# Order of three VectorE instructions and of filler matmuls in the first sample of a 16-sample attention and graph kernel

## The reference

```python
x = x + attention(_gn(x), w_qkv, w_out, b_out, gn_weight, gn_bias)
x = x + graph(_gn(x), w1, b1, gamma1, beta1, w2, b2, gamma2, beta2)

# attention, 4 heads of 32 dimensions, N = 1024 tokens
q, k, v = split(einsum('oc,bcn->bon', w_qkv, x))
q = softmax(q, axis=-2) * scale        # over the 32 dimensions of a head
k = softmax(k, axis=-1)                # over the tokens
context = einsum('bhdn,bhen->bhde', k, v)
out = einsum('bhde,bhdn->bhen', context, q)
out = normalize(einsum('oc,bcn->bon', w_out, out) + b_out) * gn_weight + gn_bias

# graph: unit vectors per token, similarity of all tokens, top 9 neighbours,
# two rounds of (feat @ w, weighted sum over neighbours, group norm, silu)
```

## Time and profile before

| what | value |
|---|---|
| median of 3 runs | 694.48 us (687.77, 694.48, 695.98) |
| profiled execution | 693.69 us, its span 691.9 us |
| mean granted TensorE clock | 0.978 of full |
| TensorE busy | 623.0 us (90%) |
| VectorE busy | 536.2 us (77%) |
| GpSimd busy | 499.6 us (72%) |
| ScalarE busy | 449.3 us (65%) |

### The profile page before, as it was taken

How to read it: one execution, slowest core, us unless ns; L and a number is a source line. 1 busy time by engine, 2 the same in 40 slices (tenths; PEclk the granted TensorE clock), 3 DMA queues, 4 the chain that set the end, 5 groups by cost and what they waited for, 6 DMA issues and landing times.

```text
span 691.9 us, 12330 instructions
## 1 busy us (share of the span) xinstructions
PE 623.0 (90%) x3821; PEld 312.0 (45%) x3821; DVE 536.2 (77%) x1008; ACT 449.3 (65%) x942; POOL 499.6 (72%) x534
## 2 busy tenths in 40 slices
PE   7787979898999999998999999998989999889984
PEld 5563635344353535353444535353534444333441
DVE  2238788888898989888898889898888988857821
ACT  2236658586786878585867768786858687643321
POOL 0122787868787888888797978888887979786810
PEclk9999999999999999999999999999999999979997
DMA  3002343434354444435353535435343634454311
GB/s 93 0 17 46 71 83 78 91 71 107 83 102 84 100 85 93 92 83 102 76 110 77 108 76 107 85 86 103 83 96 71 108 63 101 82 96 88 62 32 31
DMA packets 148722, 55.76 MB, mean 81 GB/s; under 512 B 138008, under 2 KB 138512, under 8 KB 148656
## 3 DMA queue, kind: packets, MB, share of 16 engines
q1 hardware_dynamic: 148656, 54.97, 38.8%
HBM read 12.87 MB, written 4.32 MB: 25 GB/s over the span
## 4 chain that ended last, share of the span: by engine, by line
PE 31%; POOL 25%; issue 16%; DVE 10%; DMA 9%; ACT 7%; SPq 1%; POOLq 0%; ACTq 0%; DVEq 0%
PE pC L967 17%; POOL adj L389 10%; POOL adj L384 5%; PE pS L923 4%; DMA rbc<-rn_row 4%; DMA rn_row<-rnT 4%; POOL qn L348 3%; ACT adj L527 2%; PE pB L768 2%; POOL res L407 2%; DVE kstat L607 2%; ACT ek L458 2%; PE pA L807 2%; POOL xn L372 2%; DVE top L676 2%
## 5 line engine op out<-in xcount | busy, mean ns | idle before, releaser
L967 PE MATMUL pC<-adj,xt 128*64 128x512 f32 x992 | 233.2, 603 | 3.1 <-POOL adj L395 1.8
L389 POOL TENSOR_TENSOR adj<-maskT,adj 128x128 f32<-128x128 f16 (+3 forms) x127 | 163.6, 1288 | 28.2 <-DMA maskT<-mask 25.3
L676 DVE MAX8 top<-pS 128x8 f32<-128x1024 f32 x128 | 155.6, 1224 | 30.7 <-ACT adj L527 30.5
L694 DVE MATCH_REPLACE8 mask<-top,pS 128x1024 uint16<-128x1024 f32 x128 | 155.3, 1213 | 0.0
L923 PE MATMUL pS<-xn 64*128 64x512 f32 x256 | 145.3, 655 | 6.2 <-issue 5.6
L923 PE MATMUL pS<-xn,xsw 64*128 64x512 f32 x256 | 144.7, 656 | 2.9 <-DVE mask L694 2.9
L527 ACT COPY adj<-pS 128x1024 f32<-128x1024 f32 x128 | 128.3, 1004 | 27.3 <-PE pS L925 27.1
L384 POOL TENSOR_TENSOR adj<-maskT,adj 128x128 f32<-128x128 f16 (+6 forms) x111 | 128.5, 1158 | 0.0
L967 PEld LDWEIGHTS pC<-adj,xt 128*64 128x64 f32 x992 | 63.9, 137 | 103.6 <-issue 96.0
L395 POOL TENSOR_TENSOR adj<-adj,selves 128x128 f32<-128x128 f32 x127 | 58.7, 462 | 8.7
L925 PEld LDWEIGHTS pS<-mark,place 64*128 64x128 f16 x256 | 24.5, 96 | 76.1 <-issue 76.1
(11 more groups left out here) (153 smaller groups left out, 1101.7 us busy)
## 6 DMA issues: line engine op xcount, KB each, us to landing
xs<-x SPq DMA_DIRECT2D x32, 128.0 KB, 2.8
vbc<-v_row SPq DMA_DIRECT2D x32, 128.0 KB, 2.9
rbc<-rn_row SPq DMA_DIRECT2D x30, 128.0 KB, 2.8
xsw<-xn SPq DMA_DIRECT2D x30, 128.0 KB, 2.4
out<-res SPq DMA_DIRECT2D x30, 128.0 KB, 2.4
maskT<-mask SPq DMA_TRANSPOSE x128, 3.1
cst<-packed SPq DMA_DIRECT2D x1, 471.5 KB, 3.9
y1sw<-y SPq DMA_DIRECT2D x2, 128.0 KB, 2.3
```

What stands on the lines that cost most here:

```text
L389: pool.tensor_tensor(above, m[:, r, 0:r + 1, :].bitcast(F16), above, ALU.mult).then_inc(done["upper"], 1)
L676: dve.max(top[b % 2][:, r, 0:TOP], pS[r % 2][:, :]).then_inc(done["tile_top"], 1)
L694: dve.match_replace(out=mask[n % MASKS][:, :], in_to_replace=top[b % 2][:, r, 0:TOP], in_values=pS[r % 2][:, :], imm_value=ONE_BITS).then_ ...
L967: mm = pe.matmul(ps[h * C:(h + 1) * C, 0:H], xt[:, t % NJ, t // NJ, :], adj[b % 2][:, t, h * H:(h + 1) * H], start=(t == 0), stop=(t == NT ...
```

## The change

In sample 0 VectorE's mT (scaling of the keys' product) goes behind qsum and qrec of the queries; in all other samples the order stays. Fillers: 9 in place of 8 in front of the transposes of qn of sample 0 (qT), 18 in place of 20 in front of the product with yT (ky), 8 in place of 4 in front of the sums of squares (ss).

```diff
-("ekT", 0): 9, ("qT", 0): 8, ("att", 0): 7, ("at_mean", 0): 16
+("ekT", 0): 9, ("qT", 0): 9, ("att", 0): 7, ("at_mean", 0): 16
-("k", 1): 9, ("ss", 0): 4, ("att", 1): 6
+("k", 1): 9, ("ss", 0): 8, ("att", 1): 6
-("ky", 0): 20,
+("ky", 0): 18,
...
-                yield
-                dve.wait_ge(*of("m_ps", b))
-                dve.wait_ge(*of("k_rec", b))
-                dve.wait_ge(*of("att_ps", b - 1))
-                dve.tensor_scalar(mT[:, :], pB[:, 256:256 + C], kstat[:, 2:3], SCALE, ALU.mult, ALU.mult).then_inc(done["m_copied"], 1)
+                if b >= 1:
+                    yield
+                    dve.wait_ge(*of("m_ps", b))
+                    dve.wait_ge(*of("k_rec", b))
+                    dve.wait_ge(*of("att_ps", b - 1))
+                    dve.tensor_scalar(mT[:, :], pB[:, 256:256 + C], kstat[:, 2:3], SCALE, ALU.mult, ALU.mult).then_inc(done["m_copied"], 1)
                 yield
                 dve.wait_ge(*of("q_exp", b))
                 dve.tensor_reduce(qsum[:, :], qe[:, :, :], AX.X, ALU.add).then_inc(done["q_sum"], 1)
                 dve.wait_ge(*of("q_sum", b))
                 dve.wait_ge(*of("q_norm", b - 1))
                 dve.reciprocal(qrec[:, :], qsum[:, :]).then_inc(done["q_rec"], 1)
+                if b < 1:
+                    yield
+                    dve.wait_ge(*of("m_ps", b))
+                    dve.wait_ge(*of("k_rec", b))
+                    dve.wait_ge(*of("att_ps", b - 1))
+                    dve.tensor_scalar(mT[:, :], pB[:, 256:256 + C], kstat[:, 2:3], SCALE, ALU.mult, ALU.mult).then_inc(done["m_copied"], 1)
```

More of the change, by code:

```diff
@@ L74 @@
 WARM = {
-    ("start", 0): 36, ("k", 0): 20, ("ekT", 0): 9, ("qT", 0): 8, ("att", 0): 7, ("at_mean", 0): 16, ("in_mean", 1): 6,
-    ("mi_mean", 0): 32, ("k", 1): 9, ("ss", 0): 4, ("att", 1): 6, ("sim1", 0): 2, ("mi_mean", 1): 24, ("k", 2): 9,
+    ("start", 0): 36, ("k", 0): 20, ("ekT", 0): 9, ("qT", 0): 9, ("att", 0): 7, ("at_mean", 0): 16, ("in_mean", 1): 6,
+    ("mi_mean", 0): 32, ("k", 1): 9, ("ss", 0): 8, ("att", 1): 6, ("sim1", 0): 2, ("mi_mean", 1): 24, ("k", 2): 9,
     ("xt1", 1): 24, ("g1_mean", 14): 18, ("sim7", 15): 12, ("g2_mean", 14): 18, ("g1_mean", 15): 12, ("xt2", 15): 21,
-    ("a2_0", 15): 5, ("ky", 0): 20,
+    ("a2_0", 15): 5, ("ky", 0): 18,
 }
```

## The result

The changed kernel has a median of 687.32 us over 20 runs (683.81 to 691.00), the kernel before 692.97 us over 20 runs (687.77 to 696.16). The ratio is 0.9916 with a 95% interval of 0.9894 to 0.9937: a gain of 5.8 us on 693, between 4.4 and 7.3 (the two medians themselves differ by 5.65). The time lies in the predicted range and is within 2%. The forecast of the gain was 4.0, a little under that interval.

What follows compares the result with a forecast made beforehand. The start was taken as one chain in sample 0, its queries' side held behind mT. Terms of 2.95 and 1.07 us, filler edits taken as nothing, gave 4.02 us off 693.69: 689.7 us, range 685.0 to 694.5.

Steps and rivals of the forecast that it cites:

- The chain and the free engines: Start of sample 0: one chain, queries' side late behind mT, engines idle; attention matmul expected near 25.6 in place of 29.61.
- First term: Sample 0, transposes of qn: with qsum and qrec ahead of mT they start at 23.40, not 26.35, 2.95 us earlier.
- Second term: Sample 0, transposes to attention matmul: without TensorE's idle time, sample 1's 2.19 us in place of 3.26, 1.07 us gained.
- The rival built on it: Clock at sample 0's transposes: typical executions lack the second term, only 2.95 gained, 690.7 us (691.5 from the median); chance 0.15.
- Fillers ky: Sample 0, 20 to 18 fillers before a wait that is late anyway: nothing; a clock fall would bound the loss.
- Fillers ss and the broadcasts: Sample 0, 4 to 8 fillers before the sums of squares: between -0.1 and +1.5 us at the row broadcasts, taken as 0.
- the rival that had 0.12: Sample 0's row broadcasts: the clock holds there too, 1.5 us more gained, 688.2 us; chance 0.12.
- The sum: Attention matmul of sample 0: 2.95 + 1.07 = 4.02 us earlier, all reaching the end, 689.7 us.
- the main forecast: Whole kernel: 689.7 us with its own spread of 688.5 to 691; chance 0.45.
- The shift reaches the end whole: All later samples: the last sample should still be 4.0 us ahead, since later work hangs on sample 0's attention matmul.
- The slower rival: Aggregation and similarity of a late sample, and one more place: new clock falls cost 4.4 us, 694.1 us; chance 0.08.
- tail relief: Tail, 606 to 616.5 us: shifted work may miss the clock fall there, 2.9 us more gained, 686.8 us; chance 0.14.

Runs made afterwards that it cites:

- e4: The kernel before, order untouched, with 33 in place of 8 fillers in front of the transposes of qn; ratio to before 0.9964 (0.9929 to 0.9999).
- e1: The changed kernel with the fillers in front of the sums of squares put back from 8 to 4; ratio to before 0.9930 (0.9904 to 0.9956).
- e2: The kernel before with only the fillers in front of the sums of squares raised from 4 to 8; ratio to before 1.0001 (0.9971 to 1.0031).
- e5: The changed kernel with 0 in place of 9 fillers in front of the transposes of qn; ratio to before 0.9886 (0.9853 to 0.9920).
- e6: The dose: the changed kernel with eight unused extra sums before qsum in sample 0 and 98 fillers in place of 9; median 700.35 us, ratio to before 1.0103.
- e7: The changed kernel's VectorE order with all three filler counts of before, run again with more rounds; ratio to before 0.9930 (0.9902 to 0.9959).
- f1: The changed kernel with 7 in place of 9 qT fillers and 8 new fillers in the wait before the row broadcasts; ratio to before 0.9923.
- f2: The kernel before with only 8 new fillers in the wait before the row broadcasts; one run, no ratio, 19.14 us from attention matmul to sample 1's queries.
- e3: The changed kernel's VectorE order with all three filler counts of before, first run; ratio to before 0.9946 (0.9911 to 0.9981).

## Why the prediction was right, point by point

**The chain and the free engines.** Right. The queries' side was the late one, and mT is still in time: it ends at 21.65 us, the attention matmul starts at 24.38. From the start of qe to the attention matmul the prediction's links add up to 25.59 - 18.53 = 7.06 us, and 6.99 came.

**First term, 2.95 us.** From qe to the transposes it was 26.35 - 18.53 = 7.82 and is 22.24 - 17.39 = 4.85: 2.97. That the ninth filler and not qn is late by 0.1 us holds too: qn ends at 22.08 and the transposes start at 22.24.

**Second term, 1.07 us.** From the transposes to the attention matmul 3.26 became 2.14, so 1.12, and e4, which changes only the clock, gives 1.07. Sample 1's figure was the right measure. The Trainium skill (TensorE: Matmul & The Clock Gate, Part 1) says the monitor runs free of the kernel's start. The three profiles of before fit it: the fall hits other instructions each time (transposes of 1.97, 1.09 and 1.66 us). The rival built on it, that typical executions lack the fall, is wrong: each of the five profiles with the 2.92 us wait has it, and only its place moves.

**Fillers ky: nothing.** Right; ekT is the late one as before (18.36 + 0.99 = 19.35, the eighteen fillers end at 18.78), and the clock stayed at 1.00 behind the 0.57 us of idle time.

**Fillers ss and the broadcasts: 0 taken, -0.1 to +1.5.** This is the term that was mis-sized for the change's own profile, where the broadcasts gained 1.63 us, and the rival that had 0.12, a time of 688.2, is what that profile (687.54) shows. But the reason which I gave to that rival, four fillers more just ahead, is wrong by e1 and e2. The wait in front of them is 0.90 us in all of these profiles, slow or fast, so what they cost differs by the execution; what decides it is not shown. They were slow in four of the five profiles in which the queries' side had fallen (before twice, e2, e5) and in two of seven in which it had not (e6, e7); f1 and f2, whose wait is covered, are not counted. Whether that difference is real, twelve profiles cannot say. If it is, the change brings some 0.5 x 1.6 = 0.8 us more at this place on average, an estimate from these counts.

**The sum.** Predicted 4.0 and a profiled time of 689.7; measured 5.8 (4.4 to 7.3) and 687.54. The order's 4.1 us are shown. The 687.54 lies below the 688.5 to 691 that the main forecast had as its own spread; the range holds it because it made room for the rivals with a larger gain. The average of D1 + D2 is 30.98 us over the three profiles of before and 25.83 over the two of the changed kernel, so 5.15 us; that is inside the interval. The rest of 0.65 us to the measured 5.8 is less than its uncertainty.

What was too small, by the estimate that follows, is the part of the clock: 1.07 in the second term and 0 in the fifth. Each timed run has its mean granted clock on record: on average 0.9784 in 69 runs of the kernel before and 0.9824 in 26 of the changed kernel. Counted as time at 0.50, which is 2 x (1 - clock) x span, that is an estimate of 29.8 and 24.1 us, 5.7 less (4.3 to 7.1 when the runs are resampled). A microsecond at half clock costs at most half a microsecond, so up to 2.9 us of the gain is clock. The mean times of these runs differ by 5.6; the 2.7 that is left fits the first term. The profiles show where it can come from: in the first 100 us the clock fell four times in the first profile of before (from 26.0, 46.5, 67.0 and 90.5 us) and twice in both of the changed kernel (from 60 or 61 and from 84 or 84.5 us).

**The shift reaches the end whole.** Right, shown by the dose and by D3, which over fourteen profiles is 642.5 us on average, from 639.2 to 647.7, with no tie to how early sample 1 began (correlation 0.06). D3 alone wanders over 8.5 us, about as much as the times of one kernel do and more than the whole change.

**The slower rival and tail relief.** Neither came. The tail's slow stretch is there after as before (0.51 over 10.5 us); in e1 it is about 7 us long, from 600.5 to 607.5, and what decides that stays open. Against the slower rival the prediction said that the clock was full until the tail, by the nines of the earlier trace rows, and that in some thirteen such stages a fall never happened. That was misread: a slice of that row is 17.3 us and a nine is anything from 0.90 up, so a fall of 3.5 us hides in it. The kernel before has two more, both at pieces of similarity (L923):

```profile
67.00:70.50 3.50, 3.50 (x17) 1.91 (x14) 2.24 (x5) 2.21 (x6) 2.02 (x3) 0.52 0.40 75
90.50:94.50 4.00, 3.47 (x10) 1.42 (x11) 1.74 (x6) 1.01 (x1) 4.00 (x3) 0.57 0.68 128
```

The changed kernel has them too (0.57 from 60 to 64 and from 84 to 88 us) and, in its first profile, one in a later stage:

```profile
312.50:316.50 4.00, 3.67 (x12) 1.40 (x12) 0.67 (x2) 1.01 (x1) 4.00 (x3) 0.57 0.65 121
```

The lead shrank from 6.2 to 5.0 us across it. Such a stretch is what the prediction named as a sign of being wrong. But the third profile of the kernel before has one as well (0.57 from 319 to 323 us) and the second of the changed kernel has none there, so it goes with the execution and not with the change.

## What to carry to other kernels

In the opening of a pipelined kernel, where no other sample's work covers a wait, ask of each instruction in an engine's fixed order whether the one behind it could already run: an operation that waits for the other branch may hold up the late branch for as long as its own wait. Add to the wait what the clock takes: a TensorE idle for 2.9 us paid 1.1 us more in the work behind it. Fill the short waits that remain with work only where a fall has been seen, and look further on for the fall to turn up again, as in f2. And take several profiles and the clock of all timed runs, because one execution shows a slow stretch or not by chance.

## What the runs showed of the hardware

- The same wait of 0.90 us and the same fillers gave broadcasts of 1.97 + 1.82 us in the first profile of the kernel before and 1.09 + 1.04 in the second.
- Behind a wait of 2.92 us the granted clock fell in each of five profiles, on the transposes, on the matmul behind them or on parts of both, and cost 1.1 to 1.3 us.
- After a wait of 0.82 us without fillers (e5, one profile) the granted clock fell; the eight fillers of e3 and e7 in the same place held it.
- From the start of a slow pair of broadcasts to the start of the products behind the queries (L842, L849, L852) it is 4.56 to 4.61 us in five of the six slow profiles, 4.32 in e7 and 2.99 when fast, so 1.3 to 1.6 us are lost wherever the fall begins. In e2 and the third profile of before (1.52 or 1.55, then 1.92) it begins within the first broadcast, and its end reaches into the queries (1.51 and 1.49 in place of 1.16 us).
